# A two-layer cross-attention kernel on one core: VectorE computes the row statistics of x one batch group earlier, after the query scalings, and normalises x ahead of them

## What is computed

```python
def _layernorm(x, axis=-1, eps=1e-05):
    m = jnp.mean(x, axis=axis, keepdims=True)
    v = jnp.var(x, axis=axis, keepdims=True)
    return (x - m) / jnp.sqrt(v + eps)

def _L1_xattn_ref(x1, x2, x2_mask, W, diagonal):
    x1_rep = jax.nn.relu(jnp.einsum('bld,hd->blh', x1, W))
    x2_rep = jax.nn.relu(jnp.einsum('bld,hd->blh', x2, W))
    scores = jnp.einsum('bih,bjh->bij', x1_rep * diagonal, x2_rep)
    m = (1.0 - x2_mask.astype(scores.dtype)) * NEG
    alpha = jax.nn.softmax(scores + m[:, None, :], axis=-1)
    return jnp.einsum('bij,bjd->bid', alpha, x2)

x = x + _L1_xattn_ref(_layernorm(x, axis=-1), ctx_1024, mask_BxS2_if1, L1_xattn_W, L1_xattn_diagonal)
```

## Time and profile before

| quantity | value |
|---|---|
| median of 3 executions | 602.54 us (602.17 to 604.37) |
| the profiled execution, its own time | 605.41 us |
| its span | 603.8 us |
| busy in it | PE 547.9 (91%), DVE 330.3 (55%), ACT 230.8 (38%), POOL 80.2 (13%) |
| stage C within it | about 211.4 to 264 us |

### The profile page before, as it was taken

How to read it: one execution, slowest core, us unless ns; L and a number is a source line. 1 busy time by engine, 2 the same in 40 slices (tenths; PEclk the granted TensorE clock), 3 DMA queues, 4 the chain that set the end, 5 groups by cost and what they waited for, 6 DMA issues and landing times.

```text
span 603.8 us, 8719 instructions
## 1 busy us (share of the span) xinstructions
PE 547.9 (91%) x2720; PEld 446.2 (74%) x2728; DVE 330.3 (55%) x802; ACT 230.8 (38%) x436; POOL 80.2 (13%) x121
## 2 busy tenths in 40 slices
PE   3297998978999998989999999999999999999993
PEld 2175666766888887767888878888778888788883
DVE  6566789547777778746244363353462444633332
ACT  2234455457666933336122253122252121531120
POOL 5214224114220034100000000000100001000001
PEclk9687999879999999979999999999999999999997
DMA  7665547229846677800000000000000000000001
GB/s 193 140 173 157 103 121 179 71 65 368 328 143 192 123 251 203 193 0 2 0 1 0 18 18 1 2 0 1 36 2 0 1 0 18 19 0 1 0 1 37
DMA packets 57765, 47.73 MB, mean 79 GB/s; under 512 B 37278, under 2 KB 48542, under 8 KB 57316
## 3 DMA queue, kind: packets, MB, share of 16 engines
q1 hardware_dynamic: 51960, 28.29, 17.9%
q0 software_dynamic: 5616, 18.88, 9.5%
q10 hardware_dynamic: 148, 0.04, 0.0%
HBM read 40.58 MB, written 2.10 MB: 71 GB/s over the span
## 4 chain that ended last, share of the span: by engine, by line
PE 68%; DVE 4%; issue 2%; ACT 1%; POOL 0%; DVEq 0%; ACTq 0%; POOLq 0%
PE ps L834 52%; PE ps L582 5%; PE ps L583 5%; PE ps L568 2%; PE ps L804 1%; DVE xn L1167 1%; PE ps L574 1%; PE ps L578 1%; PE ps L575 1%; ACT al L1095 1%; PE ps L818 1%; DVE sc L1407 0%; ACT h L1130 0%; DVE x L1378 0%; ACT kr L1082 0%
## 5 line engine op out<-in xcount | busy, mean ns | idle before, releaser
L834 PE MATMUL ps<-hBt,h 128*128 128x512 f32 x512 | 117.5, 390 | 0.0
L834 PE MATMUL ps<-hA,h 128*128 128x512 f32 x512 | 117.1, 390 | 0.0
L1130 ACT ACTIVATE h<-ps,scol 128x512 f32<-128x512 f32 x64 | 44.2, 690 | 175.3 <-PE ps L834 175.2
L834 PEld LDWEIGHTS ps<-hA,h 128*128 128x128 f32 x512 | 95.9, 188 | 20.2 <-DVE hA L1453 0.4
L834 PEld LDWEIGHTS ps<-hBt,h 128*128 128x128 f32 x512 | 95.8, 188 | 20.2 <-DVE hBt L1453 0.4
L834 PE MATMUL ps<-xT,w 128*128 128x512 f32 x256 | 61.6, 399 | 1.0 <-DVE h L1448 1.0
L834 PEld LDWEIGHTS ps<-xT,w 128*128 128x128 f32 x256 | 46.8, 190 | 14.5 <-issue 3.9
L1468 DVE CAST hBt<-h 128x512 fp32r<-128x512 f32 x32 | 13.7, 427 | 73.7 <-ACT h L1130 73.7
L1468 DVE CAST hA<-h 128x512 fp32r<-128x512 f32 x32 | 13.7, 427 | 70.1 <-ACT h L1130 70.1
L422 POOL TENSOR_TENSOR rstd<-ve,mhalf 128x4 f32<-128x4 f32 x16 | 16.7, 1047 | 230.9 <-DVE ve L1162 230.9
L1115 ACT ACTIVATE silD<-ps,scol 128x512 f32<-128x512 f32 x32 | 22.0, 689 | 51.5 <-PE ps L834 51.5
(11 more groups left out here) (171 smaller groups left out, 910.6 us busy)
## 6 DMA issues: line engine op xcount, KB each, us to landing
looked<-w_all_in SPq DMA_DIRECT2D x16, 704.0 KB, 5.3
h<-w_all_in POOLq DMA_DIRECT2D x16, 512.0 KB, 6.0
V<-ctx_in SPq DMA_DIRECT2D x32, 128.0 KB, 4.6
Qb<-xT SPq DMA_DIRECT2D x64, 64.0 KB, 2.1
w<-w_all_in POOLq DMA_DIRECT2D x3, 1024.0 KB, 7.8
x<-x_in SPq DMA_DIRECT2D x4, 512.0 KB, 4.5
kstA<-ctxT_in SPq DMA_DIRECT2D x4, 512.0 KB, 5.3
kstC<-ctxT_in SPq DMA_DIRECT2D x4, 512.0 KB, 5.9
```

The source lines that it names most:

```text
L834: last = mm(o, a, b, start=(k == 0 and p == 0), stop=(k == n_k - 1 and p == 1))
L1130: fn(h32[:, m % 2, :], ps[:, 2 + m % 4, :], ACT.Gelu, scale=scol[:, L + 1, m:m + 1])\
```

## The change

In stage C, VectorE's `x_stats` moves from the place before the `alT` copy to the place after `scale_queries`, and one group earlier in number: group g now makes the statistics of group g+3 there. The statistics of group 2 (n = 10) are therefore made ahead of the loop. `x_norm` of group g+2 moves in front of `scale_queries`. The number of instructions that run stays the same; the last group, and now also the third, has no statistics to make.

```diff
@@ -1382,6 +1382,7 @@
             dve.wait_ge(s["xB_done"], NB + 2)
             x_stats(2 * G + 1, Q)
             x_norm(2 * G + 1, Q)
+            x_stats(2 * G + 2, 2 * Q)
 
             def scale_queries(g):
                 for m in range(KD):
@@ -1410,18 +1411,19 @@
                     v.tensor_scalar(nmx[:, :], smx[:, :], -1.0, None, ALU.mult).then_inc(s["sm_ready"], 1)
                     x_lo(2 * G + g + 1, 1 - u)
 
-                    if u == 0:
-                        dve.wait_ge(s["xC_done"], Q * g + 2)
-                        x_stats(2 * G + g + 2, 8 - 8 * i)
-                    else:
-                        more(lambda: x_stats(2 * G + 3, 3 * Q))
                     dve.wait_ge(s["at_done"], g + 1)
                     v.tensor_copy(alT[:, :, :].rearrange("p q t -> p (q t)"), ps[:, ATB, :]).then_inc(s["at_ready"], 1)
-                    more(lambda: scale_queries(gn))
                     if u == 0:
                         x_norm(2 * G + g + 2, 8 - 8 * i)
                     else:
                         more(lambda: x_norm(2 * G + 3, 3 * Q))
+                    more(lambda: scale_queries(gn))
+
+                    def next_stats():
+                        if u == 1:
+                            dve.wait_ge(s["xC_done"], Q + 2)
+                        x_stats(2 * G + 3 + u, (3 * Q, 0)[u])
+                    if_more(dve, i, next_stats)
                     ch.step(v.reciprocal(rrs[:, :], rsm[:, :]))
                     ch.settle()
                     ch.end()
```

## The result

The changed kernel took 606.32 us (median of 17 executions, 603.63 to 610.18) against 602.25 us for the kernel before (17, 599.89 to 605.76). The ratio is 1.0063, with a 95% interval of 1.0042 to 1.0083: 2.5 to 5.0 us slower. The forecast of no change was wrong, and the time lies above the range.

A forecast was written before the change was run, and what follows sets the result against it. TensorE was taken as the bound, VectorE nearly as full; +1.5 us ahead of the loop, -1.06 in groups 0 and 1 and -0.6 in group 2 made -0.16, so 602.4 us, range 600.9 to 605.4.

The forecast's parts named there:

- The failing step: Groups 0 and 1: VectorE's fourth `xn`, due 0.01 us after GpSimd's `k_lo`, would still get their shared port.
- Rival 1: Groups 0 and 1: `k_lo` takes the port ahead of the fourth `xn`; each 0.95 us longer, total 605.3; chance 0.23.
- Ahead of the loop: Before stage C's loop: the extra `x_stats` makes the loop start 1.40 to 1.85 us later, taken as 1.5.
- `qr` path: Loop start: the scores wait for the query scalings, which come 1.40 us later, putting the first scores-plus-mask at 221.83.
- The two paths: Loop start: scores wait for the flag, its read and `turn_x` (221.26 to 222.28), and for the query scalings (221.83).
- VectorE's chain: Groups 0 and 1: VectorE's own instructions set a period of 11.58 to 11.83 us, gaining 0.53 us a group.
- Group 2: Stage C's third group, now without statistics, is paced by TensorE and gains 0.6 us, bounds 0.4 and 0.62.
- The wait of `turn_x` for `xn`: Stage C's loop: TensorE's transposes, which waited 0.90 and 0.41 us for `xn`, would follow without a wait.
- The sum: Whole kernel: +1.5 - 1.06 - 0.6 = -0.16 us, giving 602.4.
- Rival 2: Ahead of the loop: TensorE's clock falls in the new gap, costing some 2 to 3 us, about 605; chance 0.08.
- Rivals 3: Groups 0 and 1: the chain on VectorE does not bind, each gains 1.13 us, 601.2; chance 0.08.
- rival 4: End of stage C: the clock does not fall, 1.9 us and about 1 in stage D come back, 599.5; chance 0.05.

The follow-up runs named there:

- klo_later: Changed kernel with three one-element-per-partition memsets on GpSimd ahead of `k_lo` in stage C: 604.38 us, ratio 1.0018 to the kernel before.
- klo_waits: Changed kernel with GpSimd's `k_lo` in stage C waiting until the group's last `xn` is written: ratio 1.0015 to the kernel before.
- klo_halves: Changed kernel with `k_lo` of stage C as two instructions of half the size: ratio 1.0018 to the kernel before.
- both: Changed kernel with `k_lo` waiting for the last `xn` and group 2's statistics behind the first scalings: 602.23 us, ratio 0.9991 to the kernel before.
- issue_behind_root: Changed kernel with GpSimd's two weight-DMA issues of each stage C group behind `inv_root`: 607.91 us in one execution, beside 602.26 for the kernel before.
- norm_ahead_of_alT: Changed kernel with `x_norm` ahead of the `alT` copy and group 2's statistics behind the first scalings: 600.76 us, ratio 0.9968 to the kernel before.
- norm_behind_qr: Changed kernel with `x_norm` back behind the query scalings, statistics still a group ahead: ratio 1.0054 to the kernel before.

## Why the prediction was wrong

- **The failing step** is this one: "The third still runs at that point, and I think VectorE keeps the port for the fourth." The positions were right (fourth `xn` due at T + 4.83, `k_lo` at T + 4.82; measured T + 4.82 and T + 4.81 in group 0), the winner was not. `k_lo` started while the third `xn` still ran, until T + 4.91, and the fourth then took 2.52 us. Rival 1 came true in both groups: periods of 13.23 and 13.30 us against its 13.2. klo_later turned it round with 0.11 us, klo_waits took it out, klo_halves halved it; with the port free the sum is +0.22 instead of +3.22. By the rule of the Trainium skill, page "SBUF — State Buffer", section "Who interferes with whom", that the prediction weighed, the one that issues first holds the pair for its whole instruction. The page says this of VectorE's 2-port modes, which `tensor_scalar` can enter; no run here shows in which mode `xn` ran. Where the trace shows a clear lead it agrees: `k_lo` 0.15 us ahead in the changed kernel's group 1, `xn` 0.10 us ahead in klo_later. In the ties the traces do not resolve who issued first. Rows that put the two 0.01 us apart gave no ground for a chance of only 0.23.
- **Ahead of the loop**, 1.5 us was expected (bounds 1.40 to 1.85), 1.75 measured. The `qr` path was rightly counted; the rest is the gap of 0.52 instead of 0.15 us ahead of BN_AGGR. The two paths met: from `fint`'s end at 219.27 to `turn_x` at 219.79 took 0.52 of the 1.02 us allowed.
- **VectorE's chain** was predicted as 11.58 to 11.83 us with the port free; klo_waits, klo_later and both measured 11.75 to 11.80. From the mask's end to the next scores-plus-mask it takes 0.19 us, which the prediction had left between 0 and 0.25. Group 2: 0.6 predicted, 0.60 measured. The wait of `turn_x` for `xn` went as said.
- **The sum**: with rival 1 the prediction gave +2.8 us; stage C shows +3.22, 0.25 of the difference from the start and about 0.15 from the two periods. On the median before that makes 605.5 us, just over the range, whose end of 605.4 held rival 1 but not the error of its other terms. What is left up to 606.32 no run assigns.
- **Rival 2 (clock)** did not come ahead of the loop, where the granted clock stayed 1.00. It fell elsewhere, after TensorE's wait of 1.43 us until 238.02 for the softmax weights, which the long period 0 makes, for about 3 us (windows view, columns as in the earlier trace rows):

```profile
237.00:239.00 2.00, 0.92 (x3) 0.41 (x3) 1.56 (x5) 1.62 (x9) 0.00 (x0) 1.00 1.22 183
239.00:241.00 2.00, 1.85 (x5) 1.34 (x5) 1.40 (x4) 1.94 (x4) 0.00 (x0) 0.50 0.23 61
```

  TensorE was busy in 0.92 of the first 2 us; in the next 2 us its clock was at the lower level, 1.2 GHz. The matmuls at half clock were the last transpose of the softmax weights and six of the twelve of the queries. The transpose made `alT` start at T + 3.39 instead of T + 3.25, and the four `xn` with it: this is what put the fourth 0.15 us behind `k_lo` in group 1. The queries cost nothing, since their scalings wait behind the blocked `xn` until 243.57 anyway. Period 1 is 0.07 us longer than period 0. In issue_behind_root TensorE waited as long, 1.47 us, at the same place and the clock stayed 1.00; there the fourth `xn` of group 1 tied with `k_lo`, and lost as well.
- **Rivals 3 and 4** did not come: VectorE's chain did bind, and the end of stage C was as slow as before. What rival 4 describes was seen in another kernel: in klo_later the clock was granted at 1.00 from 257 to 263 us, `alT` times V took 2.00 us instead of 3.78, and stage D's first matmul came 5.63 us behind the last scores-plus-mask instead of 7.35. The edit of klo_later does not touch that part, and in klo_waits, with the same periods, `alT` times V took 3.56 us. Some of the scatter of whole executions may be this, but one trace of each kernel does not show it.

## What to carry to other kernels

An engine freed of a wait does not only run its own work earlier; others that hung on it start earlier too, here `k_lo`, because `inv_root` no longer stood in front of it. When a move brings two instructions that share a port within a tenth of a microsecond of each other, treat the price of losing as at least as likely as the gain (here VectorE lost all eight ties), and move one of them off the other by order, not by luck. Put moved work where its engine waits for another one (behind the first scalings, in the wait for the queries), and count the chain once more: with the changed order two of the three periods were bound by VectorE even with the port free (11.8 us), and it took another order (norm_ahead_of_alT) to bring them to the 11.1 us that TensorE allows.

## What was not expected of the hardware

- Two TENSOR_SCALAR forms of VectorE wait for GpSimd's subtraction: `xn` (128x256, one input in SBUF and two per-row scalars, 0.32 us apart when free) and `ve` (128x4, 0.17 us alone, 1.07 beside `k_lo`). BN_STATS (1.39 us for four) and BN_AGGR (0.38) do not in norm_ahead_of_alT, nor does `qr`, whose input is in PSUM (0.75 at 226.91, beside the `k_lo` of the earlier trace rows).
- The winner of the port changed with a shift of 0.11 us. `k_lo` did not have to wait visibly for the `xn` in progress in group 0 (2.38 us long, as when alone); when it came 0.24 us before that `xn` ended, in group 1, it took 2.47. The loser waited as one long instruction (2516 ns for a 128x256 TENSOR_SCALAR), so a group's mean hides it; the four instructions' total of 3.48 us is what shows.
- The 0.37 us of extra gap ahead of BN_AGGR appeared in all kernels in which `x_stats` followed `x_norm` directly ahead of the loop, and in none in which another instruction stood between them there. Adjacency alone does not make it: inside the loop of norm_behind_qr `x_stats` follows `x_norm` directly, and the gap is 0.14 us (229.79 + 1.40 to 231.33). Its cause stays open.
